# Attention in a fused four-layer kernel: row-group matmuls with scores computed twice, in place of masked queries and transposed weights

## The reference

```
Q = x @ W_Q.T / sqrt(8);  K = x @ W_K.T;  V = x @ W_V.T       # per head h: 8 columns
S[i, j] = Q[i] . K[j] + slope[h] * (j - i)      for j <= i, else masked
slope[h] = 256 ** (-(h + 1) / 16)
x = layernorm(x + softmax(S) @ V @ W_O.T)
```

## Time and profile before

| | |
|---|---|
| median of three runs | 1690.85 us |
| time of the profiled execution | 1694.99 us |
| its span (first to last instruction) | 1693.2 us |
| mean granted clock of TensorE | 0.852 |
| PE / PEld / DVE / ACT / POOL busy | 1281.7 / 965.0 / 951.2 / 592.8 / 263.8 us |
| DMA moved | 111.58 MB |

### The profile page before, as it was taken

One profiled execution on the slowest core, in us unless ns is written; L12 is line 12 of the kernel. 1 busy time (PEld: TensorE's weight loads), 2 busy tenths in 40 slices (PEclk: granted clock), 3 DMA queues, 4 the chain that ended last, 5 costly groups with the idle time before them and its releaser, 6 DMA issues. The chain is left out here.

```text
span 1693.2 us, 34235 instructions
## 1 busy us (share of the span) xinstructions
PE 1281.7 (76%) x11002; PEld 965.0 (57%) x11002; DVE 951.2 (56%) x3327; ACT 592.8 (35%) x1531; POOL 263.8 (16%) x280
## 2 busy tenths in 40 slices
PE   6999998999988113533699777699817897979782
PEld 4999996566645113510466452355405897979772
DVE  3666665344423776656645668444586265656423
ACT  3555552222220201132122121133311375757562
POOL 3322210000000000000000000222020343434332
PEclk9999998999999565666799878699957598989896
DMA  6996000000000000000172001333180121212111
GB/s 246 367 357 242 0 0 1 29 19 19 10 1 1 1 1 2 2 0 0 43 152 51 6 1 41 89 103 100 34 278 1 53 58 37 59 35 58 43 42 55
DMA packets 93077, 111.58 MB, mean 66 GB/s; under 512 B 13888, under 2 KB 66071, under 8 KB 92304
## 3 DMA queue, kind: packets, MB, share of 16 engines
q1 hardware_dynamic: 85200, 100.87, 19.7%
q0 software_dynamic: 7760, 9.25, 1.8%
HBM read 61.14 MB, written 53.43 MB: 68 GB/s over the span
## 5 line engine op out<-in xcount | busy, mean ns | idle before, releaser
L1654 PE MATMUL m_psY<-large,m_hT 128*128 x992 | 142.4, 288 | 4.8 <-issue 2.5
L1640 PE MATMUL m_psH<-m_xT,m_up 128*128 128x128 f32 x992 | 139.7, 286 | 0.0
L1654 PEld LDWEIGHTS m_psY<-large,m_hT 128*128 128x128 f32 x992 | 129.8, 195 | 5.6 <-issue 5.5
L1640 PEld LDWEIGHTS m_psH<-m_xT,m_up 128*128 128x128 f32 x992 | 129.3, 203 | 0.1
L1580 POOL DMA_INDIRECT rows<-m_ys,m_slot x93 | 90.4, 972 | 132.2 <-DVE m_slot L1848 117.3
L815 DVE SCALAR_TENSOR_TENSOR m_hid<-m_psU,m_wu,m_sg 128x512 f32<-128x512 f32 x64 | 48.1, 751 | 92.2 <-ACT m_sg L802 92.2
L1299 PE MATMUL m_acc<-se_place,se_parts 128*128 128x512 bf16 x384 | 89.5, 384 | 0.0
L1697 ACT ACTIVATE m_up<-large 128x512 f32 x124 | 78.1, 630 | 28.6 <-DVE m_valid L1751 17.2
L802 ACT ACTIVATE m_sg<-m_psG,m_wu 128x512 f32<-128x512 f32 x64 | 44.0, 687 | 123.3 <-PE m_psU L764 123.3
L424 ACT ACTIVATE at_Pr<-at_S,at_nmax 128x128 f32<-128x128 f32 x128 | 51.4, 402 | 98.8 <-DVE at_nmax L380 98.6
L776 PEld LDWEIGHTS m_psD<-m_wd,m_hid 128*128 128x128 f32 x512 | 67.0, 191 | 31.3 <-issue 30.4
(11 more groups left out here) (537 smaller groups left out, 2898.5 us busy)
## 6 DMA issues: line engine op xcount, KB each, us to landing
rows<-blank SPq DMA_DIRECT2D x2, 19584.0 KB, 103.2
m_xs<-rows SPq DMA_DIRECT2D x124, 76.5 KB
large<-in_L_attn_firs SPq DMA_DIRECT2D x4, 2048.0 KB, 16.6
large<-comb_rows SPq DMA_DIRECT2D x64, 128.0 KB, 5.2
se_wu<-in_L_ffn_up SPq DMA_DIRECT2D x32, 192.0 KB
W2T<-in_L_ffn_down_turned SPq DMA_DIRECT2D x1, 4096.0 KB, 12.5
large<-in_L_ffn_up SPq DMA_DIRECT2D x4, 1024.0 KB, 8.1
large<-in_L_ffn_down SPq DMA_DIRECT2D x16, 256.0 KB, 6.9
```

What stands on the lines that cost most here:

```text
L1640: m = nc.tensor.matmul(psH[b][:, c * P:(c + 1) * P], up[b][:, c * P:(c + 1) * P], xT[b][:], start=True, stop=True)
L1654: m = nc.tensor.matmul(psY[b][:, 0:wide], hT[b][:, c * P:(c + 1) * P], k.W2[:, bass.ds(e + c * WIDE, wide)], start=(c == 0), stop=(c == C ...
```

## The change

The mask and the transposes go. Instead:

- **Row groups.** Four heads are laid at partitions 0, 32, 64 and 96 of the tiles QA and KA. A head has 8 rows of Q or K, a ninth row that carries slope times key position (against ones), and a tenth with minus the row's maximum. A score matmul reads 9 or 10 partitions of one 32-row group of the PE array. QA and KA are filled by 32 DMAs, each of 8 partitions x 2048 columns, half issued by SP, half by ACT.
- **Scores twice.** A first pass (`scores`, on top of the causal mask that `hide_later` puts into PSUM as bfloat16) serves only the maximum, which one DVE `tensor_reduce` takes. The maxima are turned by two small matmuls, copied by ACT, and put into row 9 of QA by four DMAs a sequence. A second pass (`dots`) computes the scores turned, keys on partitions, so that the exponential comes out in the layout that the product with V needs. The first pass runs 26 heads (`LEAD`) ahead of the second.
- **Slopes.** The part of the slope that goes with the key's place in its tile is a bias of the exponential and a factor on V (`at_weight`); V gets a ninth kind of column, ones, which gives the sums. POOL clears what lies above the diagonal in each exponential tile.
- **Product with V.** `weigh` has V as the stationary side (128 rows x 32 columns, four heads in four column groups) and the exponentials as the moving side.
- **Moves.** Everything is unrolled: there is no loop any more. Weight loads and constant tiles go into `setup_stage`; the filter loads go to the end of SP's list in `experts_stage`; `clear_rows` goes to the first block of `delta_scan`, on SP.

```diff
 setup_stage
+            for w, n in ((k.at_wq, "Q"), (k.at_wk, "K"), (k.at_wv, "V"), (k.at_wo, "O")):
+                sp.dma_start(w, a[f"L0_attn_W_{n}"]).then_inc(k.tally("at_w_in").sem, 16)
+            sp.wait_ge(*sloped.at(1))
+            sp.dma_start(k.at_slope[:], k.at_row[:].rearrange("p (i g) -> p i g", i=4))...
+            nc.gpsimd.memset(k.at_QA[:], 1.0).then_inc(made.sem, 1)
+            for h in range(HEADS):
+                m = nc.vector.memset(k.at_row[:, h % 4 * 4 + h // 4:h % 4 * 4 + h // 4 + 1], float(slopes[h]))
...
+            nc.vector.memset(k.at_KA, 1.0)
 attention_stage, SP
+                sp.wait_ge(*q_out.at(4))
+                for g in range(GROUPS):
+                    for i in range(TILES):
+                        rows, head = slice(32 * i, 32 * i + HD), slice(32 * g + HD * i, 32 * g + HD * (i + 1))
+                        sp.dma_start(QA[rows, g, :], QT[head, :]).then_inc(rows_in[g].sem, 16)
                 start_delta_loads(k, a, sp)
+                for b in range(BATCH):
+                    sp.wait_ge(*peak_out.at(b + 1))
+                    for g in range(GROUPS):
+                        sp.dma_start(QA[9:P:32, g, b * SEQ:(b + 1) * SEQ], peakT[4 * g:4 * g + 4, b % 2, :])...
 attention_stage, POOL
+                nc.gpsimd.tensor_tensor(VA[:, :, :, 0:18], VA[:, :, :, 0:18], ..., ALU.mult)
+                for v in range(ALL):
+                    pool.wait_ge(*expd.at(v + 1))
+                    nc.gpsimd.affine_select(out=diag(PT[:, v % PRING]), ...)   # 128 x 256
 attention_stage, PE
+                def hide_later(u):
+                    if u >= TILES:
+                        pe.wait_ge(*reduced.at(u - TILES + 1))
+                    nc.tensor.matmul(diag(out), identb[:], maskb[:].unsqueeze(1).to_broadcast([P, 2, P]), ...)
+                def scores(u, part):     # part 0: 256 columns, part 1: 128 columns
+                    rows = slice(r, r + 9)
+                    if part == 0:
+                        return nc.tensor.matmul(psS[:, u % TILES, P:CAUSAL], QA[rows, g, keys(b, 1)],
+                                                KA[rows, g, b * SEQ:(b + 1) * SEQ], ...)
+                def dots(v, part):       # the same turned, into psT[:, v % TRING]
...
+                def weigh(q):
+                    pe.wait_ge(*cleared.at(4 + TILES * (q + 1)))
+                    for kt in range(2):
+                        for i in range(TILES):
+                            m = nc.tensor.matmul(o, VA[:, 2 * b + kt, h, :], x, ...)   # o: 32 partitions
+                for step in range(-LEAD // 2, ALL // 2 + 4):
+                    us = [u for u in (2 * step + LEAD, 2 * step + LEAD + 1) if 0 <= u < ALL]
+                    vs = [v for v in (2 * step, 2 * step + 1) if 0 <= v < ALL]
+                    for u in us:
+                        hide_later(u)
+                    for v in vs:
+                        if v >= TRING:
+                            pe.wait_ge(*expd.at(v - TRING + 1))
+                    for part in range(2):
+                        for u in us:
+                            scores(u, part)
+                        for v in vs:
+                            dots(v, part)
 attention_stage, ACT
+                for g in range(GROUPS):
+                    for i in range(TILES):
+                        act.dma_start(KA[rows, g, :], KT[head, :]).then_inc(rows_in[g].sem, 16)
+                    nc.scalar.activation(PT[:, v % PRING, :, :]..., psT[:, v % TRING, 0:CAUSAL], ACT.Exp, bias=...)
 attention_stage, DVE
+                for u in range(ALL):
+                    dve.wait_ge(*scored.at(u + 1))
+                    nc.vector.tensor_reduce(peaks[:, b % 2, n, :], psS[:, u % TILES, 0:CAUSAL]..., AX.X, ALU.max)
 experts_stage (first layer), SP
+            more_sp(sp)          # start_fir_loads: 4 DMAs of 2 MB
 delta_scan, first block
+            @block.sync
+            def _(sp):
+                clear_rows(k, sp)
```

More of the change, by code:

```diff
@@ L101, in setup_stage @@
     loaded.close(16)
-    made.close(3)
+    made.close(6)
+    sloped.close(2)
+    k.tally("x_in5").close(16)
     turned.close(4)
@@ L224, in _ @@
+        slopes_in = k.tally("x_in4")
+        peak_in = [k.tally(f"x_in{5 + i}") for i in range(2)]
+        ps_cm = nc.psum_tensor("at_ps", [P, 8, 512], F32)
+        with ps_cm as ps, nc.Block() as block:
+            psS, psT, psO = ps[:, 0:4, :], ps[:, 4:7, :], ps[:, 7, :]
+            diag = lambda t: t[:, 0:3:2, :]
+            keys = lambda b, kt: slice(b * SEQ + kt * P, b * SEQ + (kt + 1) * P)
             @block.sync
             def _(sp):
-                for t, w in ((wq, w_q), (wk, w_k), (wv, w_v), (wo, w_o)):
-                    sp.dma_start(t[:], w).then_inc(w_in.sem, 16)
@@ new lines, in copy_peaks @@
+                def copy_peaks(b):
+                    act.wait_ge(*turned.at(b + 1))
+                    if b >= 2:
+                        act.wait_ge(*peak_in[b % 2].at(64 * (b // 2)))
+                    nc.scalar.activation(peakT[:, b % 2, :], psO[0:HEADS, SEQ:2 * SEQ], ACT.Copy).then_inc(peak_out.sem, 1)
+                copy_peaks(0)
+                for v in range(ALL):
+                    act.wait_ge(*dotted.at(v + 1))
+                    if v >= PRING:
+                        act.wait_ge(*weighted.at((v - PRING) // TILES + 1))
+                    nc.scalar.activation(PT[:, v % PRING, :, :].rearrange("p x c -> p (x c)"),
+                                         psT[:, v % TRING, 0:CAUSAL], ACT.Exp,
+                                         bias=k.at_bias[:, v % HEADS:v % HEADS + 1]).then_inc(expd.sem, 1)
+                    b, n = divmod(v, HEADS)
+                    if n == 2 * TILES - 1 and b + 1 < BATCH:
+                        copy_peaks(b + 1)
+                    ended = b - 1 if n == TILES - 1 else (b if v == ALL - 1 else -1)
+                    if ended >= 0:
+                        act.wait_ge(*weighted.at(GROUPS * (ended + 1)))
+                        nc.scalar.activation(raw[:, ended % 2, :], psO[:], ACT.Copy).then_inc(raw_out.sem, 1)
@@ L430, in attention_stage @@
+                for b in range(ended, BATCH):
+                    norm(b)
+        project_and_add_stage(k, "at", O, QT, wo)
         w_in.close(64)
-        biased.close(3)
         masked.close(3)
         projected.close(12)
-        proj_out.close(4)
-        v_out.close(4)
+        q_out.close(4)
+        k_out.close(4)
+        v_out.close(8)
+        cleared.close(4 + ALL)
+        for t in (scored, reduced, dotted, expd):
+            t.close(ALL)
+        for t in (peaked, turned, peak_out, normed, raw_turned, raw_out):
+            t.close(BATCH)
@@ L438, in project_and_add_stage @@
+        weighted.close(QUADS)
+        for t in rows_in:
+            t.close(128)
+        slopes_in.close(64)
+        for t in peak_in:
+            t.close(64 * BATCH // 2)
+    k.at_room.close()
 def project_and_add_stage(k, name, O, OT, w, w_in_dram=None):
```

369 lines of the change are left out of this document (196 added, 173 removed).

## The result

The changed kernel takes 1715.31 us (median of 4 runs, 1711.32 to 1721.73); the kernel before, timed beside it, 1690.71. The ratio is 1.0149, with an interval of 1.0113 to 1.0185: slower, by 1.5%.

A forecast was written before the change was run, and what follows sets the result against it. PE was taken as the bound. Attention ending at 169 instead of 256.7 us (−88) and the scan's +8 summed to −80: 1615 us from the profiled 1694.99, 1611 against the median, range 1578 to 1658.

The forecast's parts named there:

- I take 0.9: Attention: PE's granted clock taken as 0.9 at some 75% busy, adding 0.05 us a head.
- the clock stays at half: Rival, attention: steps of 2.2 and 3.2 us, attention ending at 231, kernel at 1673 us; chance 0.07.
- the granted clock in attention is under 0.8: Attention: one of the signs named in advance that would show the prediction wrong.
- I take 0.64: Attention's score passes: four row groups work at once, so a two-head step's matmuls take 0.64 us, against 2.57 without overlap.
- no overlap: Rival, attention: row groups do not overlap at all, 2.06 us a head with the mask, kernel at 1735 us; chance 0.07.
- overlap in part: Rival, attention: row groups' weights load one after another, 1.33 us a head, kernel at 1657 us; chance 0.11.
- 1.0 us a head: Attention: steps of 1.41 and 1.80 us, plus sequence chains and clock, give 1.0 us a head, range 0.8 to 1.33.
- the first scores start at 27.5: Attention's start: after projections end at 22, 16 row transfers a queue at 0.43 us each and 2.0 to landing.
- `dots` start at 43: Attention's start: the turned second pass begins at 43 us, once the first maxima are turned, copied and landed.
- DVE's 0.55 plus waits, 15 us: Attention's start: the first pass's lead of 26 heads goes at DVE's pace and takes 15 us.
- I take 1 us for eight, 8 us: Delta scan: `clear_rows` slows some eight instruction fetches by 1 us each, 8 us in all, bounds 0 and 25.
- the rival at 0.13: Rival, delta scan: it pays 25 us for `clear_rows`, attention as forecast, kernel at 1628 us; chance 0.13.

The follow-up runs named there:

- c3: Changed kernel with both score passes reading all 32 rows of a row group, the further rows holding ones; 1637.2 us, ratio 0.9744 to the kernel before.
- c7: Changed kernel with 32-row score matmuls, `clear_rows` in the filter stage, row transfers in two parts, delta loads after the first maxima; 1626.30 us, ratio 0.9608 to the kernel before.
- c5: Kernel before with only `clear_rows` moved, out of attention into the first delta-scan block; 1714.72 us, ratio 1.0115 to the kernel before.
- c1: All stages left out; PE alone runs blocks of 256-column float32 matmuls in several forms; four 9-row groups take 0.80 us a round at half clock.
- c4: Changed kernel with 9 and 10 rows kept, plus one unused whole-array 128 x 128 float32 matmul a head; 1679.01 us, ratio 1.0005 to the kernel before.

## Why the prediction was wrong

The forecast was 1611 us and the median is 1715.31, 104 us more. The profiled execution (1711.32) is 96 us over the sum's 1615, and these 96 are taken apart here, by the prediction's own steps:

- **The clock ("I take 0.9").** This failed. PE was at "some 75% busy" in the forecast and at 96% in fact, and yet at 0.50. The rows behind the step, 0.74 at 61% busy and 1.00 at 100%, mixed busy share with form: the 1.00 came from whole-array matmuls, the 0.74 from a stretch of 32x32 tiles, and no row had row groups that were a quarter full. The rival "the clock stays at half" named the event, at 0.07; it was held unlikely because "here gaps stay under 1 us", and they did, and the clock fell all the same. Of the signs of being wrong, "the granted clock in attention is under 0.8" is what happened. c3 alone gives back 58 us. The rival's price for the loop was right: from first turned matmul to the end it had 231 − 43 = 188 us, and 257.8 − 69.0 = 189 were measured.
- **Overlap of row groups ("I take 0.64").** Right. Records start 10 to 20 ns apart, and a step's streams take 1.60 us at half clock. The rivals of no overlap and of overlap in part fell; the kernel came out slower by another mechanism than theirs.
- **Steps and rings ("1.0 us a head").** Right at full clock: c3 has 3.74 us for four heads, 0.94, with PE waiting 0.50 us on ACT. From first turned matmul to last product c7 takes 182.4 − 54.4 = 128 us, and the forecast had 169 − 43 = 126. Part of this is luck: steps forecast at 1.41 and 1.80 us take 1.76 and 1.98 (0.94 a head against 0.80), while 128 heads at 0.94 leave at most 8 us for the chains at the sequences' ends, forecast at 0.16 a head, 20 in all.
- **The beginning ("the first scores start at 27.5", "`dots` start at 43").** It failed by 26 us, in two terms. The 0.43 us an issue and 2.0 to landing came from a weight load of 128 rows of 512 bytes; these transfers have 8 rows of 8 KB, 0.77 to 0.82 an issue, and the 512 KB of a group take 6.5 us. With the rows early (c7) first scores come at 25.7. "DVE's 0.55 plus waits, 15 us" for the lead was 35 here, with the later groups' rows in it, and 29 in c7: 2.12 us a step at half clock, 1.17 at full, which over 13 steps makes 12 of the 14. The Trainium skill (DMA: Bandwidth & Descriptors, Rules for kernel authors) says that an outermost dimension below 16 confines a transfer to at most as many of the 16 DMA engines. The trace agrees: the outermost dimension is 8 here, and from 24 to 34 us, before the delta loads are issued, the engines' mean share is 0.52, about 8 of 16, against 0.70 beside those loads (36 to 46 us) and 1.01 under `clear_rows`; no run changed that dimension.
- **`clear_rows` in the scan ("I take 1 us for eight, 8 us").** The mechanism was right, the size was not: six gaps with 3.1 us more each, 18.5, inside the bound of 25 and nearest to the rival at 0.13. c5 puts the whole at 20 us. SP's issue took 47.5 us there, not 62.55, so the barrier never waited for it.
- **The filters' load** cost nothing, as forecast.

With terms: attention +89 to the forecast (26 to the first turned matmul, 63 behind it), the scan +12, the rest −5, together 96. The chance of slower was 0.07. No case let two rivals hold at once, though they don't exclude one another: half clock (1673), the costly scan (17 more) and the start that nobody doubted (26) make 1716 (1711 with the scan as measured).

## What to carry to other kernels

Cutting an array into row groups was worth its parallelism here only with the groups full: PE at 96% busy with 9 rows of 32 ran at half clock for most of the loop, and reading all 32 rows, of which 22 hold nothing but ones, gave 58 us for no work. Read the granted clock beside the busy share in every stretch, and take a clock for a forecast only from a row of the same form of matmul. A large transfer without a reader was not free beside the scan, whose engines leave short loop iterations: put it in a stage whose engines stream through their program, and send of few long rows first the part that is read first.

## What the runs showed of the hardware

- Four row groups of 9 rows with nothing else brought the clock to 0.50 and kept it there (45 to 69 us in c1). In the changed kernel, with masks and V products among them, it was 0.50 from 100 to 125 us and 1.00 from about 81 to 92. Four row groups of 32 rows, four column groups and four 32x32 tiles held 1.00 in c1; one row group of 32 alone fell to 0.50.
- Matmuls that add work can make a kernel faster: c4 is 1.4% faster than the changed kernel.
- Six gaps of PE in the scan, read as program loads, took 1.1 to 1.9 us with the DMA engines idle, 4.0 to 5.0 beside the clearing at 353 GB/s and 3.8 to 5.2 in c5.
- A cast of 128x128 from SBUF to SBUF on DVE, where another took 0.24 us just before, took 6.91 us from 13.26 on, as long as a memset of 8192 on POOL that began at 13.17. It cost nothing here, and no run took it apart:

```profile
13.17 6.92 POOL L282 MEMSET large<- 128x8192 f32 x1
13.26 6.91 DVE L467 CAST at_maskb<-at_mask 128x128 bf16<-128x128 f32 x1 [0.28 <-POOL at_mask L280]
```
